# Two graph attention layers on one core: scores, projection, transposes, output projection, values in each step

## The chip, the core and the metric

The kernel runs on one core of a Trainium2 chip. The time is device microseconds of that core from one launch. Five engines work side by side and meet only through semaphores: TensorE (PE; its weight loads are shown as PEld) multiplies matrices into PSUM, VectorE (DVE), ScalarE (ACT) and GpSimd (POOL) do the rest, and SyncE (SP) issues the DMAs. Each engine takes its own instructions strictly in the order in which they are written.

## The reference, cut to what matters

128 graphs, 128 nodes each, 256 features, 8 heads of 32, float32. Two layers, each a masked attention over the nodes of a graph:

```python
# layer 0
nx = _ln(x, ln1_g, ln1_b)
q, k, v = nx @ wq + bq, nx @ wk + bk, nx @ wv + bv          # heads of 32
bias = jnp.where(adj > 0, 0.1 * adj * adj, -jnp.inf)[:, None]
attn = softmax(einsum('bhqd,bhkd->bhqk', q, k) / sqrt(32) + bias)
x1 = x + (einsum('bhqk,bhkd->bhqd', attn, v) @ wo + bo)
x  = x1 + gelu(_ln(x1, ln2_g, ln2_b) @ w1 + b1) @ w2 + b2    # 256 -> 1024 -> 256
# layer 1
q, k, v = x @ Wq + bq, x @ Wk + bk, x @ Wv + bv
attn = softmax(where(adj == 0, -inf, q k^T * scale))
y = x + (attn v) @ Wo + bo
out = (y - mean) * rsqrt(var + eps) * gamma + beta
```

## The kernel before, in words

The 128 graphs are worked on in 32 groups of four. Three stages run at once in one turn of a loop: A (layer 0's attention) of group n, M (the two-layer perceptron of layer 0) of group n-1, and C (layer 1) of group n-2. Turns 0, 1, 31, 32 and 33 are written out, the 29 between are a hardware loop. A turn has eight steps. Each step k computes the scores of one unit, that is one graph of one stage: steps 0 to 3 the four units of C, steps 4 to 7 the four of A. The rest of a unit's work follows in later steps, behind the scores of others. `lags` (line 61) says by how many steps: the transposes T of the probabilities one step later, the values V and the output projection W two steps later. A negative number is a unit of the previous turn.

What TensorE does in a step, in `body` (line 1399): the scores (`make_scores`, 16 small matmuls on 32 rows each, into `p_heads`), V of the unit two back (16 small matmuls 32 columns wide, stationary values, moving `probs_t`), the step's first projection ("early" and "mid": q, k or v of stage A or C, or the up-projection), T of the first four heads (`turn(.., 0)`), W of the unit two back, T of the other four heads, then "ahead" (the transposes XT of x before a projection) and "fill" (the second projection). Float32 products of the projections are three passes over a high and a low part of each operand (`three_passes`, line 1225, the multiply at line 1233). In step 3 the projection is the up-projection (UP, eight chunks of six matmuls) and half of DOWN, in step 4 the other half of DOWN.

The other engines, in the same step. VectorE (`body`, line 1060): adds the mask to the scores and takes the row bound (`mask_scores`, L925, eight instructions), inverts the sums of the exponentials (`invert`, L936), makes the low part of V's result (`heads_low`, L1005), adds W to the residual (`add_residual`, L1015), copies T's second half to `probs_t` (`turned`, L999), then the statistics of the layer norm (`measure`, L818 to L826) and, a step or more later, the normalised row (`apply_norm`, L832). ScalarE (`body`, line 752): V's high part (`heads_high`, L749), exps in two halves of four heads (L692), the copies of the projections, T's first half (L744), the high part of transposed x (L713). GpSimd (`body`, line 605): the multiply of the exponentials by the inverted sums (`make_probs`, L614, two halves), rstd (L560), the bias adds (`add_bias`, L592; the one into `res_c` at step 0 waits until all stores of the previous group are through), gamma and beta (`finish`, L601, L603). SyncE's stores of a finished unit wait for L603.

T writes the same PSUM banks as the scores, so each half of T waits until the masks of the newest scores in its banks are done, and for `make_probs`. Scores wait until the copies of earlier T are done. The four `p_bank`s are handed out in turn; each use waits until the use four before it is emptied (`take`, line 1207).

XT "M" in step 2 transposes the normalised `x_two` for the perceptron and needs all four of the turn's units through `apply_norm`: before, W of the last of them (A's unit 3) is in step 1.

Of the kernel before, what the change touches and what calls it, by code (L numbers as in the profile page):

```python
# [35 lines left out]
P = 128  # L36
# [3 lines left out]
HD = D // H  # L40
# [19 lines left out]

def lags(steps, pending, drain):
# [12 lines left out]
class Shape:  # L74
# [3 lines left out]
    def __init__(self, it, stages, following, before, drain):  # L78
# [10 lines left out]
        self.lag, self.tail = lags(self.steps, pending, drain)  # L89


        self.late, waiting = {}, [-3] if pending else []
# [24 lines left out]
        if it == NG:  # L117
            for table in (self.mid, self.fill, self.early):
                for k in (5, 6, 7):
                    table.pop(k, None)  # L120
            self.tail = self.tail[:3] + [("XH", "C", 0)] + self.tail[3:]
            self.ahead[4], self.fill[4] = [("KH", "C", 0), ("XH", "C", 1)], [("QH", "C", 0), ("KH", "C", 1)]
# [17 lines left out]
        for k in range(STEPS):  # L140
            lag = self.lag.get(k, [])
            self.number(self.first.get(k, []) + only("V", lag) + self.early.get(k, [])
                        + self.mid.get(k, []) + only("W", lag) + self.ahead.get(k, []) + self.fill.get(k, []))
# [8 lines left out]
        assert not self.looped or len(self.use) % BANKS == 0  # L152

# [37 lines left out]
class Turn:  # L191
# [32 lines left out]
    def high(self, key):  # L224

        return self.grown(self.s.high0 + self.s.high[key] + 1, len(self.s.high))
# [18 lines left out]
def build(nc, T, out):  # L245
    ctx = ExitStack()
    with ctx:
# [28 lines left out]
        piece_rooms = [sb(f"piece_room{i}", [P, 2, TOK]) for i in range(4)]  # L276
        scaled_rooms = [sb(f"scaled_room{i}", [P, 2, TOK]) for i in range(2)]
# [157 lines left out]
        def turned_rows(g):  # L435

            return probs_t[:, HC * g:HC * (g + 1)].rearrange("p (a h) n -> p a (h n)", a=2)
# [5 lines left out]
        def made(t, kind, what, i):  # L443
# [5 lines left out]
            return t.bank((kind, what, i), earlier=(what == "C" and not here))  # L449

# [14 lines left out]
        def _(sp):  # L465
# [36 lines left out]
            def body(t):  # L502
# [26 lines left out]
                if s.c:  # L529
                    store(t, 0)  # L530
                    store(t, 1)
# [3 lines left out]
                if s.c:  # L535
                    store(t, 2)
# [14 lines left out]
        def _(pool):  # L551
# [53 lines left out]
            def body(t):  # L605
                s = t.s
                setup_over(pool, t)
                for k in range(STEPS):
# [35 lines left out]
                    rstd_of(t, s.lag.get(k, []))  # L644
# [26 lines left out]
        def _(act):  # L671
# [69 lines left out]
            def turned(t, r):  # L741
                u, _, _ = t.unit(r)
                act.wait_ge(probs_turned, u * KC + 1)
                nc.scalar.activation(turned_rows(0), turned_columns(0), ACT.Copy).then_inc(turned_out0, 1)  # L744

            def heads_high(t, r):
                bank, number = t.bank(("O", r))
# [4 lines left out]
            def body(t):  # L752
                s = t.s
                setup_over(act, t)
                for k in range(STEPS):
# [19 lines left out]
                    for op in s.ahead.get(k, []):  # L775
                        evacuate(t, op)
                    for op in s.fill.get(k, []):
# [21 lines left out]
        def _(dve):  # L799
# [196 lines left out]
            def turned(t, r):  # L996
                u, _, _ = t.unit(r)
                dve.wait_ge(probs_turned, u * KC + 2)
                nc.vector.tensor_copy(turned_rows(1), turned_columns(1)).then_inc(turned_out1, 1)  # L999

            def heads_low(t, r):
                bank, _ = t.bank(("O", r))
                dve.wait_ge(high_made, t.high(("O", r)))
# [56 lines left out]
            def body(t):  # L1060
                s = t.s
                setup_over(dve, t)
                for k in range(STEPS):
                    lag = s.lag.get(k, [])
                    for op in s.first.get(k, []):
                        evacuate(t, op)
                        second_piece()
                    if k in s.units and k != s.behind:
# [3 lines left out]
                    for _, r in only("V", lag):  # L1072
# [18 lines left out]
                    for _, r in only("W", lag):  # L1091
                        add_residual(t, r)
                    for _, r in only("T", lag):
                        turned(t, r)
# [356 lines left out]
```

## Time and profile before

| | |
|---|---|
| median of 3 runs | 2177.07 us (2175.8 to 2178.03) |
| profiled execution | 2175.24 us, its span 2173.4 us |
| granted TensorE clock, mean | 0.998 |
| PE / PEld busy | 2138.1 us (98%) / 1853.7 us (85%) |
| DVE / ACT / POOL busy | 1802.9 (83%) / 1683.4 (77%) / 1153.3 us (53%) |
| 16 DMA engines | 75.76 MB, mean 35 GB/s |

A timeline row gives start, length, engine, line, operation, the tiles it writes and reads, and the count of merged instructions; the length runs to the end of the last one, which overlaps with the start of the next group. For the length of a TensorE group the difference of two starts is therefore used. A bracket at the end is idle time of the engine before the row, with what ended it.

### The profile page before, as it was taken

Reading aid. Unit: us, or ns where it says so; the run is one execution under the profiler, and the core shown is the slowest. Engines: PE = TensorE matmul, PEld = TensorE weight load, DVE = VectorE, ACT = ScalarE, POOL = GpSimd, SP = SyncE. Lnnn points to the kernel's source line nnn. Section 1 sums busy time; section 2 is a strip of 40 time slices with the busy share of each in tenths; the row PEclk is TensorE's granted clock in tenths of the full one; section 3 lists DMA queues with packets and bytes.
Section 4 is the critical chain, followed back from the end, with each engine's and each line's share of the span. In section 5 each row is a group of like instructions: output and inputs, shape, how many; then the busy total and the mean of one; then the engine's idle time right before and its main releaser. Section 6 shows DMA issues by size and latency. Waiting matters only on the chain.

```text
span 2173.4 us, 59064 instructions
## 1 busy us (share of the span) xinstructions
PE 2138.1 (98%) x20372; PEld 1853.7 (85%) x20372; DVE 1802.9 (83%) x8415; ACT 1683.4 (77%) x5658; POOL 1153.3 (53%) x1264
## 2 busy tenths in 40 slices
PE   8899999999999999999999999999999999999997
PEld 6888888888888888888888888888888888888876
DVE  7788888888888888888888888888888888888785
ACT  5678887778787778877787877787777788777875
POOL 4545555445655445555455554456554555544554
PEclk9999999999999999999999999999999999999999
DMA  4010111010111001111101110101111011101000
GB/s 130 30 33 26 40 33 40 26 35 28 40 33 40 24 29 38 34 40 31 31 28 41 33 40 26 35 28 40 33 32 32 27 40 33 40 27 34 19 26 18
DMA packets 94310, 75.76 MB, mean 35 GB/s; under 512 B 8129, under 2 KB 93761, under 8 KB 94017
## 3 DMA queue, kind: packets, MB, share of 16 engines
q1 hardware_dynamic: 94016, 71.99, 10.9%
q8 instruction: 167, 2.74, 0.5%
q14 instruction: 127, 1.03, 0.2%
HBM read 55.20 MB, written 16.78 MB: 33 GB/s over the span
## 4 chain that ended last, share of the span: by engine, by line
PE 96%; DVE 2%; ACT 1%; issue 1%; DMA 0%; POOL 0%; SPq 0%; POOLq 0%; DVEq 0%; ACTq 0%
PE p_bank L1233 67%; PE p_heads L1367 10%; PE p_heads L1354 8%; PE p_bank L1386 7%; PE p_bank L1266 4%; ACT scores L692 1%; DVE probs_t L999 0%; DVE normed L952 0%; PE p_bank L1156 0%; DMA scores<-in_L_gnn_wk 0%; DVE x_two L832 0%; DVE scores L925 0%; SPq L469 0%; DVE normed L946 0%; PE p_heads L1156 0%
## 5 line engine op out<-in xcount | busy, mean ns | idle before, releaser
L692 ACT ACTIVATE scores<-scores,negmax 128x128 f32<-128x128 f32 x2048 | 793.8, 392 | 23.3 <-DVE negmax L925 23.0
L614 POOL TENSOR_TENSOR scores<-scores,inverse 128x512 f32<-128x512 f32 x512 | 541.0, 1062 | 324.4 <-DVE inverse L936 324.4
L692 ACT ACTIVATION_READ_ACCUMULATOR scores<-scores,negmax 128x1 f32 x2048 | 391.9, 191 | 0.0
L1233 PEld LDWEIGHTS p_bank<-w_down,hidden 128*128 128x128 f32 x3072 | 374.6, 190 | 8.5 <-issue 5.9
L1233 PE MATMUL p_bank<-w_down,hidden 128*128 128x256 f32 x3072 | 381.8, 284 | 0.0
L1233 PE MATMUL p_bank<-normed,w_up 128*128 128x512 f32 (+1 forms) x1584 | 369.3, 389 | 3.6 <-DVE normed L946 2.9
L1233 PEld LDWEIGHTS p_bank<-normed,w_up 128*128 128x128 f32 x1584 | 286.2, 188 | 67.0 <-issue 10.2
L1367 PE MATMUL p_heads<-ident,scores 128*128 128x128 f32 x2048 | 309.7, 274 | 5.9 <-DVE negmax L925 3.3
L925 DVE CUSTOM_DVE_ANT_0 scores<-p_heads,adj_a 128x128 f32<-128x128 f32 x1024 | 235.2, 286 | 41.2 <-issue 41.2
L1367 PEld LDWEIGHTS p_heads<-ident,scores 128*128 128x128 f32 x2048 | 239.0, 140 | 31.6 <-DVE negmax L925 11.0
L735 ACT ACTIVATE p_bank<-p_bank,ready_cols 128x512 f32<-128x512 f32 x248 | 164.2, 662 | 126.9 <-PE p_bank L1233 121.5
L925 DVE CUSTOM_DVE_ANT_0 scores<-p_heads,adj_c 128x128 f32<-128x128 f32 x1024 | 233.2, 286 | 30.8 <-issue 30.8
L1233 PE MATMUL p_bank<-w_o,heads_t 128*128 128x256 f32 x1536 | 245.9, 296 | 2.4 <-DVE heads_t L1005 2.4
L749 ACT ACTIVATE heads_t<-p_bank 128x256 fp32r<-128x256 f32 x256 | 98.3, 384 | 159.6 <-PE p_bank L1386 159.5
L986 DVE TENSOR_TENSOR hidden<-p_bank,hidden 128x512 fp32r<-128x512 f32 x248 | 171.5, 691 | 60.6 <-ACT hidden L739 54.6
L744 ACT ACTIVATE probs_t<-p_heads 128x512 f32<-128x512 f32 x256 | 149.8, 585 | 87.2 <-PE p_heads L1367 87.2
L1233 PE MATMUL p_bank<-normed,w_k 128*128 128x512 f32 (+1 forms) x780 | 209.4, 404 | 4.2 <-DVE normed L952 2.6
L1233 PE MATMUL p_bank<-normed,w_q 128*128 128x512 f32 (+1 forms) x780 | 210.8, 406 | 0.0
L1233 PE MATMUL p_bank<-w_v,normed 128*128 128x256 f32 x1536 | 210.3, 287 | 0.0
L560 POOL TENSOR_TENSOR rstd_A<-spread_A,half 128x4 f32<-128x4 f32 x32 | 32.5, 1017 | 333.7 <-DVE spread_A L826 333.6
L1233 PEld LDWEIGHTS p_bank<-w_o,heads_t 128*128 128x128 f32 x1536 | 199.0, 190 | 3.2 <-DVE heads_t L1005 3.0
L1233 PEld LDWEIGHTS p_bank<-w_v,normed 128*128 128x128 f32 x1536 | 187.0, 189 | 12.5 <-issue 12.1
(130 smaller groups left out, 3708.1 us busy)
## 6 DMA issues: line engine op xcount, KB each, us to landing
res_a<-in_x SPq DMA_DIRECT2D x32, 512.0 KB, 3.8
out<-res_c SPq DMA_DIRECT2D x128, 128.0 KB, 1.7
x_in<-in_x SPq DMA_DIRECT2D x31, 512.0 KB, 3.9
adj_a<-in_adj SPq DMA_DIRECT2D x32, 256.0 KB, 2.9
adj_c<-in_adj SPq DMA_DIRECT2D x32, 256.0 KB, 2.9
piece_room<-in_L_gnn_w SPq DMA_DIRECT2D x2, 512.0 KB, 8.1
x_two<-in_x SPq DMA_DIRECT2D x1, 512.0 KB, 5.4
res_c<-in_L_gnn_w SPq DMA_DIRECT2D x1, 512.0 KB, 6.2
```

Source lines behind the costliest of these rows:

```text
L614: nc.gpsimd.tensor_tensor(rows_g, rows_g, inverse[:, step % 2, heads].unsqueeze(2).broadcast_to([P, HC, P]), ALU.mult).then_inc(probs_made, 1)
L692: last = nc.scalar.activation(scores[:, k % 2, h], scores[:, k % 2, h], ACT.Exp, scale=-1.0, bias=negmax[:, k % 2, h:h + 1], accum_out=tot ...
L735: nc.scalar.activation(src[:, :], src[:, :], ACT.Gelu, bias=ready_cols[:, 8 + j:9 + j]).then_inc(gelu_made, 1)
L744: nc.scalar.activation(turned_rows(0), turned_columns(0), ACT.Copy).then_inc(turned_out0, 1)
L749: nc.scalar.activation(heads_t[:, HI].rearrange("p c n -> p (c n)"), p_bank[bank][:, 0:KC * P], ACT.Copy).then_inc(high_made, 1)
L925: nc.vector.tensor_tensor_reduce(out=scores[:, k % 2, slot], in0=score_columns(c, j), in1=adj[stage][:, b, :], scale=1.0, scalar=LARGEST, ...
L986: nc.vector.tensor_tensor(hidden[:, j, LO, :], src[:, :], hidden[:, j, HI, :].bitcast(F32), ALU.subtract).then_inc(drained[bank], 1)
L1233: last = nc.tensor.matmul(dst, stationary(i), moving(j), start=(n == 0), stop=(n == total_n - 1))
L1266: last = nc.tensor.transpose(dst[:, b * P:(b + 1) * P], src[:, b, c * P:(c + 1) * P], ident[:, :])
L1354: last = nc.tensor.matmul(score_columns(c, j), queries[room(t, stage)][rows_j, c, tokens], keys[room(t, stage)][rows_j, c, tokens], start= ...
L1367: last = nc.tensor.transpose(turned_columns(g)[:, n // 2, (n % 2) * P:(n % 2 + 1) * P], scores[:, par, HC * g + n, :], ident[:, :])
L1386: last = nc.tensor.matmul(dst[HD * j:HD * (j + 1), c * P:(c + 1) * P], values[room(t, stage)][:, b, h * HD:(h + 1) * HD], probs_t[:, slot_ ...
```

## The change

From turn 1 to turn 32 the order of a step is another one (`later_lags`, `Shape.later`, `Shape.products`). T is still one step behind, V two, W now three. TensorE's order in a step is: scores, the step's projections, both halves of T together, W of the unit three back, V of the unit two back. Steps 2, 3, 4 and 7 differ where the transposes of x or the perceptron are in them (`products`). Since V of a unit now comes after T of the next one, the turned probabilities lie in two rooms, by the parity of the unit; the second is `piece_room0`, which is used only while weights are loaded. `heads_t` is written at the start of the step after V. In step 2 VectorE adds, measures and normalises A's unit 3 at once, and GpSimd's rstd comes ahead of `make_probs`. SyncE issues the load of `res_a` ahead of the stores 0 and 1. Turn 33 and turn 0 keep the old order.

```diff
+def later_lags(steps, pending, drain):
+    by_step = {}
+    for r, k in enumerate(steps):
+        by_step[k] = [(op, r - n) for op, n in (("T", 1), ("W", 3), ("V", 2)) if r >= n or pending]
+    last = len(steps) - 1
+    tail = [("T", last), ("W", last - 2), ("V", last - 1), ("XH", "C", 0), ("W", last - 1),
+            ("V", last), ("W", last)] if drain else []
+    return by_step, tail
...
+        self.later = before is not None and it != NG + 1
+        self.lag, self.tail = (later_lags if self.later else lags)(self.steps, pending, drain)
-        self.late, waiting = {}, [-3] if pending else []
+        self.late, waiting = {}, [-4] if pending else []
...
+    def products(self, k):
+        early, mid, ahead, fill = (x.get(k, []) for x in (self.early, self.mid, self.ahead, self.fill))
+        turns, outs, heads = (only(op, self.lag.get(k, [])) for op in "TWV")
+        if k == 2:
+            return early + outs + fill + turns + ahead + heads
+        if k == 3:
+            return mid + turns + outs + heads + ahead + fill
+        if k == 4:
+            return early + turns + ahead + outs + heads + fill
+        return ahead + early + mid + fill + turns + outs + heads
...
+        probs_rooms = [probs_t, piece_rooms[0][:, :, :].rearrange("p a (h n) -> p (a h) n", n=P)]
...
+        def turned_room(t, r):
+            return probs_rooms[0 if t.s.before is None else r % 2]
...  SyncE
-                if s.c:
-                    store(t, 0)
-                    store(t, 1)
                 if s.a and s.before is not None:
                     sp.wait_ge(*drained_use(t, ("DOWN", 1)))
                     sp.dma_start(res_a[:, :, :], ...)
                 if s.c:
+                    store(t, 0)
+                    store(t, 1)
                     store(t, 2)
...  GpSimd
+                    if k == 2 and s.later:
+                        rstd_of(t, s.lag.get(k, []))
                     if k in s.units and k != s.behind:
                         make_probs(k, 0)
...  ScalarE
-                    for _, r in only("V", lag):
+                    for r in split_first(s, k):
                         heads_high(t, r)
+                    for op in s.ahead.get(k, []) if s.later and k == 7 else []:
+                        evacuate(t, op)
...
+                    for op in s.fill.get(k, []) if s.later and k not in (3, 4) else []:
+                        evacuate(t, op)
                     for _, r in only("T", lag):
                         turned(t, r)
+                    for _, r in only("V", lag) if s.later and k == 3 else []:
+                        heads_high(t, r)
+                    for op in s.ahead.get(k, []) if s.later and k == 2 else []:
+                        evacuate(t, op)
                     if k in s.units and k != s.behind and not long:
                         exps(t, k, 1)
...  VectorE
+                    heads_lead = s.later and k == 2
+                    for r in split_first(s, k) if heads_lead else []:
+                        heads_low(t, r)
...
+                    if k == 2 and s.later:
+                        for _, r in only("W", lag):
+                            add_residual(t, r)
+                            measure(t, r)
                     if k == 2:
                         for r in s.late.get(k, []):
-                            apply_norm(t, r, GB - 1)
+                            apply_norm(t, r, GB - 2)
+                    for op in s.ahead.get(k, []) if s.later and k == 7 else []:
+                        evacuate(t, op)
...
+                    if s.later:
+                        if k == 2:
+                            for _, r in only("W", lag):
+                                apply_norm(t, r, GB - 1)
+                        for _, r in only("T", lag):
+                            turned(t, r)
+                        for op in s.ahead.get(k, []) if k in (2, 4) else []:
+                            evacuate(t, op)
+                        for _, r in only("W", lag) if k != 2 else []:
+                            add_residual(t, r)
+                        for _, r in only("V", lag) if k == 3 else []:
+                            heads_low(t, r)
...  TensorE
+                    if s.later:
+                        for op in s.products(k):
+                            if op[0] == "T":
+                                turn(t, op[1], 0)
+                                turn(t, op[1], 1)
+                            elif len(op) == 2 and op[0] in "VW":
+                                lagging(t, *op)
+                            else:
+                                work(t, op)
```

## Rows read from the trace of the kernel before

**Rows 1.** The page, first part: busy time, share of the span, instructions.

```profile
PE 2138.1 (98%) x20372; PEld 1853.7 (85%) x20372; DVE 1802.9 (83%) x8415; ACT 1683.4 (77%) x5658; POOL 1153.3 (53%) x1264
```

**Rows 2.** Waits of TensorE: engine, line, for whom; us, times, longest.

```profile
PE p_heads L1354 <- DVE probs_t L999: 3.7, 3, 1.7
```

**Rows 3.** Timeline of TensorE, step 0 to the scores of step 1.

```profile
238.83 0.73 PE L1354 MATMUL p_heads<-keys_c,queries_c 32*128 32x128 f32 x16
239.49 0.65 PE L1386 MATMUL p_bank<-probs_t,values_a 128*32 128x128 f32 x16
240.06 1.65 PE L1233 MATMUL p_bank<-normed,w_k 128*128 128x512 f32 x6
241.55 0.60 PE L1367 MATMUL p_heads<-ident,scores 128*128 128x128 f32 x4
241.91 0.96 PE L1233 MATMUL p_bank<-w_o,heads_t 128*128 128x256 f32 x6
...
243.06 1.64 PE L1233 MATMUL p_bank<-normed,w_k 128*128 128x512 f32 x6
244.63 0.73 PE L1354 MATMUL p_heads<-keys_c,queries_c 32*128 32x128 f32 x16
```

**Rows 4.** Timeline of TensorE, the same group in two turns.

```profile
130.44 8.50 PE L1233 MATMUL p_bank<-normed,w_up 128*128 128x512 f32 x36
...
196.55 8.50 PE L1233 MATMUL p_bank<-normed,w_up 128*128 128x512 f32 x36
```

**Rows 5.** Timeline of TensorE, DOWN after scores (turn 1) and ahead of values (turn 32).

```profile
79.59 6.01 PE L1233 MATMUL p_bank<-w_down,hidden 128*128 128x256 f32 x48
...
2118.95 5.91 PE L1233 MATMUL p_bank<-w_down,hidden 128*128 128x256 f32 x48
2124.80 0.64 PE L1386 MATMUL p_bank<-probs_t,values_c 128*32 128x128 f32 x16
```

**Rows 6.** Timeline of TensorE, values and projection in step 5.

```profile
221.10 0.64 PE L1386 MATMUL p_bank<-probs_t,values_c 128*32 128x128 f32 x16
221.79 1.62 PE L1233 MATMUL p_bank<-normed,w_k 128*128 128x512 f32 x6
```

**Rows 7.** Timeline of VectorE, step 7: first mask, residual add, statistics, spread.

```profile
299.10 0.29 DVE L925 CUSTOM_DVE_ANT_0 scores<-p_heads,adj_a 128x128 f32<-128x128 f32 x1 [0.65 <-issue]
...
302.36 0.42 DVE L1015 TENSOR_TENSOR res_a<-p_bank,res_a 128x256 f32<-128x256 f32 x1 [0.57 <-PE p_bank L1233]
...
303.41 0.42 DVE L818 BATCH_NORM_STATS2 stats_M<-res_a 128x6 f32<-128x256 f32 x1
...
304.08 0.15 DVE L826 TENSOR_SCALAR spread_M<-moments_M 128x1 f32<-128x1 f32 x1
```

**Rows 8.** Timeline of GpSimd, end of step 7 and step 0.

```profile
304.31 0.55 POOL L560 TENSOR_TENSOR rstd_M<-spread_M,half 128x1 f32<-128x1 f32 x1 [0.16 <-DVE spread_M L826]
304.83 1.28 POOL L592 TENSOR_TENSOR res_c<-x_two,row_bias 128x512 f32<-128x512 f32 x1
306.91 1.04 POOL L614 TENSOR_TENSOR scores<-scores,inverse 128x512 f32<-128x512 f32 x1 [0.80 <-DVE inverse L936]
```

**Rows 9.** Timeline of GpSimd and VectorE at the end of turn 0.

```profile
54.86 0.55 POOL L560 TENSOR_TENSOR rstd_M<-spread_M,half 128x1 f32<-128x1 f32 x1 [2.49 <-DVE spread_M L826]
55.37 2.39 POOL L398 TENSOR_TENSOR w_down<-x_in,w_down 128x1024 fp32r<-128x1024 f32 x1
...
55.44 2.47 DVE L832 TENSOR_SCALAR x_two<-res_a,moments_M,rstd_M 128x256 f32<-128x256 f32 x1 [0.66 <-POOL rstd_M L560]
```

**Rows 10.** Groups by line, ScalarE: busy us, mean ns; idle before, releaser.

```profile
L692 ACT ACTIVATE scores<-scores,negmax 128x128 f32<-128x128 f32 x2048 | 793.8, 392 | 23.3 <-DVE negmax L925 23.0
L713 ACT ACTIVATE normed<-p_bank 128x512 fp32r<-128x512 f32 x188 | 100.7, 588 | 40.4 <-PE p_bank L1266 40.4
```

**Rows 11.** Timeline of GpSimd, step 6: gamma of layer 1's last unit.

```profile
297.16 0.74 POOL L601 TENSOR_TENSOR res_c<-res_c,gamma 128x256 f32<-128x256 f32 x1
```

**Rows 12.** The page, DMA issues: count, KB, median us to landing.

```profile
out<-res_c SPq DMA_DIRECT2D x128, 128.0 KB, 1.7
```

More of the change, by code:

```diff
@@ L141, in __init__ @@
             lag = self.lag.get(k, [])
-            self.number(self.first.get(k, []) + only("V", lag) + self.early.get(k, [])
-                        + self.mid.get(k, []) + only("W", lag) + self.ahead.get(k, []) + self.fill.get(k, []))
+            if self.later:
+                self.number(self.products(k))
+            else:
+                self.number(self.first.get(k, []) + only("V", lag) + self.early.get(k, [])
+                            + self.mid.get(k, []) + only("W", lag) + self.ahead.get(k, []) + self.fill.get(k, []))
             if k == self.steps[-1]:
@@ L222, in normed_room, with high @@
         return (self.it + (what in "MN" or not self.s.m and self.s.c)) % 2
-    def high(self, key):
-        return self.grown(self.s.high0 + self.s.high[key] + 1, len(self.s.high))
+    def high(self, key, earlier=False):
+        s = self.s
+        n = s.before.high[key] - len(s.before.high) if earlier else s.high[key]
+        return self.grown(s.high0 + n + 1, len(s.high))
 def run_pipeline(eng, shapes, body):
@@ L449, in made, with split_first, out_use, out_high @@
             return t.bank((kind, what, i), earlier=(what == "C" and not here))
+        def split_first(s, k):
+            if s.later and k == 4:
+                return []
+            return [r for _, r in only("W" if s.later else "V", s.lag.get(k, []))]
+        def out_use(t, r):
+            taken_here = r >= 0 or ("V", r) in [op for ops in t.s.lag.values() for op in ops]
+            return t.bank(("O", r)) if taken_here else t.bank(("O", r + len(t.s.before.order)), earlier=True)
+        def out_high(t, r):
+            if r >= 0 or ("O", r) in t.s.high:
+                return t.high(("O", r))
+            return t.high(("O", r + len(t.s.before.order)), earlier=True)
         def second_turn(t):
@@ L643, in body @@
                         add_bias("A", res_a_loaded, (t.group_a + 1) * 16, 1, 1)
-                    rstd_of(t, s.lag.get(k, []))
+                    if k != 2 or not s.later:
+                        rstd_of(t, s.lag.get(k, []))
                     if k == 3 and second_turn(t):
@@ L1071, in body @@
                         invert(t, k - 1, 1)
-                    for _, r in only("V", lag):
+                    for r in split_first(s, k) if not heads_lead else []:
                         heads_low(t, r)
@@ L1097, in body @@
                             evacuate(t, op)
-                    for _, r in only("W", lag):
+                    for _, r in only("W", lag) if not (s.later and k == 2) else []:
                         measure(t, r)
-                    if k == 1:
-                        for r in s.late.get(k, []):
-                            apply_norm(t, r, 2)
-                    for op in s.ahead.get(k, []):
+                    for op in s.ahead.get(k, []) if not (s.later and k in (2, 4, 7)) else []:
                         evacuate(t, op)
@@ L1408, in body @@
                         make_scores(t, k)
+                    if s.later:
[5 more added lines that the diff above has]
+                                lagging(t, *op)
+                            else:
+                                work(t, op)
+                        for op in s.tail if k == s.steps[-1] else []:
+                            if len(op) == 2 and op[0] in "TVW":
+                                lagging(t, *op)
+                            else:
+                                work(t, op)
+                        continue
                     for op, r in only("V", lag):
```

34 lines of the change are left out of this document (17 added, 17 removed).

## The prediction

> **What bounds the kernel now.** First the page's busy shares: TensorE's matmuls are busy 98% of the span [rows 1]; the chain that ended last is nearly all TensorE too. Then the list of who waited for whom, for TensorE: its longest entry is 3.7 us in the whole run, in three waits, all in the last turns [rows 2]. Then the timeline of a step: TensorE's groups follow each other without an idle gap [rows 3]. And the period: the 36 UP matmuls that start at 130.44 come again at 196.55 [rows 4], 66.1 us later, and so on through the loop. So the time is the length of TensorE's own stream. Other engines matter only when they make it stop, and today they hardly do. A change of order can therefore win only what changing from one kind of matmul to another costs, and loses every wait that it creates.
>
> I count from the profiled execution: 2175.24 us, span 2173.4. The median of the timed runs is 1.8 us higher; I add that at the end.
>
> **The price of changing the kind.** An ordinary step is scores S (0.66), values V (0.57), six large matmuls K (1.49), transposes T (0.355), output projection W (0.80), T, K (1.57 with the first of them after T) [rows 3]. K unhindered is 1.38 (half of the 2.86 that twelve take). So K after V pays 0.11, and K ahead of S 0.09. T and W change places at next to nothing: 0.355 + 0.80 is what ten such matmuls take in a row. S and V are tiled (32 rows; 32 columns), and entering or leaving them is what costs; the change S to V pays about 0.11 + 0.02 of the same kind. DOWN directly after S lasts 6.01, 0.10 longer than after UP (5.91): entering the full array costs the same after S as after V. And those 48 matmuls, 0.12 each, take 5.85 up to the V that follows them [rows 5], 0.09 of it for leaving, as ahead of S. So leaving costs about 0.1 whatever follows, and entering belongs to what is entered.
>
> With that the new steps come out so. Old: full array to S, S to V, V to full: three changes. New: S to full, full to V, V to next S: again three, and by the rows above the same 0.55 us. Only step 3 (S, UP, T, W, V, UP, DOWN) has one more exit and entry: 0.2 us a turn. Merged transposes save 0.005 eight times, step 7 enters x transposes instead of a projection after S (0.05 less), and in step 5 today's wait of K for the split of x (V group 0.69 instead of 0.57 [rows 6]) goes, 0.12. Sum: 0.2 - 0.04 - 0.05 - 0.12, nothing. The one change that no row shows is V to S. Its bounds: free (0.21 less, seven times a turn) to 0.1 more; I take it as S to V, the nearest row.
>
> The Trainium skill, TensorEngine Tiling (Array Packing), Key Properties, says that changing the tiling mode, not just the tile, drains the engine. By it V to S is such a change as well, and the ring stays equal; this trace shows the drain at S to V and at V to full.
>
> **Step 2: a new wait.** W of a turn's last layer-0 unit moves from step 1 to step 2, and the transposes of x (X) in the same step need that unit normalised. Counted from the start of step 2's scores: S 0.66, first half of v 1.48, so W runs 2.14 to 2.85; second half 1.37, eight transposes 0.87 (0.109 each, four T take 0.355 up to W and 0.08 more of its first): X could start at 5.10. VectorE: step 1's measuring now comes after W, at step end, and is over at 0.9; ScalarE's and its own part of the heads 0.4 each; masks start near 1.4 and eight of them at 0.21 with a reciprocal end at 3.2. Residual add 0.42, statistics to spread 0.82 (303.41 to 304.08 + 0.15) [rows 7], spread ready at 4.5. GpSimd starts rstd 0.08 later and takes 0.55 [rows 8], 0.67 with VectorE on a normalise: 5.2. Then comes the collision. GpSimd's next instruction is the multiply of step 2's first four heads, 1.04 [rows 8], whose reciprocals VectorE has made at 5.0, and it starts back to back; VectorE's normalise needs the rstd and starts 0.07 later. The end of turn 0 shows just this [rows 9]: rstd to 55.41, GpSimd's next from 55.37 for 2.39, VectorE's normalise from 55.44 for 2.47 instead of 0.41: it ended 0.15 after GpSimd. So here it ends at 5.2 + 1.04 + 0.15 = 6.4, X starts at 6.44, and TensorE stands **1.3 us**. Without the collision: 5.27 + 0.41 + 0.06 = 5.74, 0.64 us. If VectorE runs half a microsecond ahead of my count the latter shrinks to 0.1; behind it, 1.6. I take 1.3.
>
> The Trainium skill, SBUF — State Buffer, section "SBUF: two separate sides", calls the port pair of VectorE and GpSimd an exclusive lock, held for the whole instruction by whichever starts first. By that rule the wait is 1.3, without it 0.64; the trace agrees, 2.47 us at 55.44.
>
> **Step 3.** ScalarE now copies x (two copies of 0.59, overlapping to 1.09) [rows 10] before the second half of step 2's exps. From X's start x0: copies 0.86 to 1.95, four exps at 0.39 plus a last read, to 3.55, heads high 0.3, heads low 0.36, so step 3's masks run 4.24 to 6.0. TensorE: V starts x0 + 1.04, V 0.57, S 0.66, UP 2.86, first four transposes 0.44, second four at 5.57; these write the banks that the masks read. **0.5 us**, between 0 and 0.8. Before, the same transposes came after W, at the scores' start + 5.2, and the masks ended at 3.9. UP needs x's split at x0 + 2.27 and has it at 2.2: nothing.
>
> **Step 0.** The last layer-1 unit is now projected in step 6 and finished by GpSimd in step 7, where before it had step 6 for that [rows 11]. From step 7's scores: ScalarE copies x_in to 2.65, exps to 4.25, GpSimd's multiply 4.55 to 5.65, gamma and beta 0.75 each to 7.2, bias of res_a 1.28 to 8.45, rstd 0.55 to 9.0; the store of res_c lands at 7.25 + 1.7 to 2.0 [rows 12]. The bias add into res_c waits for that store: 9.0 to 10.4 (1.28) [rows 8], and only then comes the multiply for the second four heads, 11.4. Step 7 lasts 6.6, so it is ready 4.8 after step 0's scores start; the second four transposes would go at 0.66 + 2.86 + 0.44 = 3.96. Before, it was ready at 306.91 + 1.04 = 307.95, 3.0 after scores at 304.95, for transposes at 3.87. **0.8 us**, between 0 (everything 0.8 earlier) and 1.2.
>
> **Edits that cost nothing.** The second room for turned probabilities is memory that is idle after the start. S waits for the copies of turned probabilities; VectorE's starts 0.2 after the transposes (4.6) and ends at 5.3, scores at 5.8: 0.4 spare, covered by W and V. The residual add and the measuring then end at 0.8 of the next step, just when its masks can start (0.80 after the scores, [rows 7], scores at 298.30); any more would move the masks, whose user (3.96) is 0.9 behind their end. In step 4 W and V stand between the transposes of x and the next scores and hide the split. SP's queue: the res_a load is moved ahead of two stores that now finish later; it is needed in step 5. The banks of W and V are free a step ahead. Turn 32 has no projections to hide step 2's chain: 3 us once. The last turn keeps the old order.
>
> **Sum.** Steps 0 and 2 in 30 turns: 30 x (0.8 + 1.3) = 63; step 3 in 31 turns 15.5; turn 32 3: 81.5 us. 2175.2 + 81.5 = 2256.7, and with the 1.8 of the median 2258; I give 2255.
>
> **The rivals.**
> A, chance 0.30: part of it. The waits in steps 0 and 3 come out hidden, because a wait in one place gives every engine time to catch up for the next, and VectorE gets the ports first in step 2: 31 x 0.64 = 20, to 31 x (1.3 + 0.5) = 56. 2185 to 2232, middle 2205. For it: my chains have three to six terms each, and an error of 0.3 in VectorE's start removes half a wait. Against: at 55.4 the same two engines met in the same order [rows 9].
> B, chance 0.09: the waits are all hidden and the ring is equal: 2177. For it: today's VectorE has some 0.65 idle ahead of masks [rows 7]. Against: step 2's chain has 2.4 us of fixed latency from W's end, against 2.25 us of TensorE's work.
> C, chance 0.13, the other side: V to S is free, both being tiled. Place: seven of eight step borders. Price 0.21 each, 1.5 us a turn, 46 us. It decides from where the waits are less than 1.5 us a turn: with step 2's 0.64 alone 2177 + 20 - 46 = 2151; with all of mine, 2.6 a turn, even it leaves the kernel slower. Against: at S to V, also between two tiled kinds, the full price stands.
> The forecast has 0.48, own range 2232 to 2285.
>
> What a measurement can tell from no change is about 0.2%, 4.4 us. Faster 0.13 (C), same 0.09 (B), slower 0.78 (forecast, A). The range must reach from the forecast over A to B to leave out no more than C and a little above: 2174 to 2285.
>
> **What would show it.** In the profile after: TensorE's waits should name x_two's normalise (L832) before the transposes of x, some 30 times at 1.3; negmax before transposes in step 3 at 0.5; GpSimd's scores multiply before transposes in step 0 at 0.8, with GpSimd's res_c add waiting for a store. The step 2 normalise should last about 1.1 instead of 0.41. The turn should be 68.7 us. A V group that is 0.57 long with S right behind shows the equal price; 0.45, rival C. If the turn is 66.1 and no such waits are listed, my schedule of VectorE and GpSimd is wrong, not the prices.

## The result, and the profile after

The changed kernel takes 2265.81 us (median of 4 runs, 2264.55 to 2267.68) against 2177.55 us (4 runs, one more than in the table ahead of the prediction, 2175.8 to 2179.3) beside it: ratio 1.041, 95% interval 1.0397 to 1.0422, 88 us slower. The profiled execution has a span of 2265.9 us at a mean granted clock of 0.991.

The page of the changed kernel, first part (answers to [rows 1]):

```profile
PE 2169.0 (96%) x20372; PEld 1876.7 (83%) x20372; DVE 1851.6 (82%) x8415; ACT 1684.1 (74%) x5658; POOL 1155.8 (51%) x1264
```

The first entries of TensorE's list of waits (engine, line, for whom; us, times, longest; answers to [rows 2]):

```profile
PE p_bank L1347 <- DVE x_two L894: 34.3, 32, 2.2
PE p_heads L1448 <- issue: 24.5, 32, 1.9
PE p_heads L1448 <- DVE negmax L987: 10.3, 37, 1.1
```

The number of instructions is that of before on every engine. TensorE's share of the span fell by two points only, and the page alone would hide where 88 us went. The list of waits has it: before, the longest entry was 3.7 us in three waits; now three entries have a wait in nearly every turn (32, 32 and 37 times), 69 us in sum. L1347 is the transposes of x, L894 the normalise; L1448 the transposes of probabilities, L987 the masks. The entry in the middle is step 0's wait. The list puts it down to "issue", that is, to nothing that the profile shows, and not to GpSimd's multiply of the probabilities, as the prediction expected; that the multiply is the cause rests on the rows and edits told at e2 and e5.

Timeline of TensorE in the changed kernel, steps 2 and 3 of one turn:

```profile
953.08 1.04 PE L1448 MATMUL p_heads<-ident,scores 128*128 128x128 f32 x8
955.16 1.09 PE L1347 MATMUL p_bank<-ident,x_two 128*128 128x128 f32 x8 [1.04 <-DVE x_two L894]
956.19 0.64 PE L1467 MATMUL p_bank<-probs_t,values_c 128*32 128x128 f32 x16
956.76 0.73 PE L1435 MATMUL p_heads<-keys_c,queries_c 32*128 32x128 f32 x16
957.54 3.00 PE L1314 MATMUL p_bank<-normed,w_up 128*128 128x512 f32 x12
960.38 0.60 PE L1448 MATMUL p_heads<-ident,scores 128*128 128x128 f32 x4
961.17 0.66 PE L1448 MATMUL p_heads<-ident,scores 128*128 128x128 f32 x4 [0.19 <-DVE negmax L987]
961.59 0.96 PE L1314 MATMUL p_bank<-w_o,heads_t 128*128 128x256 f32 x6
...
963.05 8.52 PE L1314 MATMUL p_bank<-normed,w_up 128*128 128x512 f32 x36
```

The same, step 0 of the next turn, and the UP group one turn later (answers to [rows 3] and [rows 4]):

```profile
1005.11 0.73 PE L1435 MATMUL p_heads<-keys_c,queries_c 32*128 32x128 f32 x16
1005.77 3.03 PE L1314 MATMUL p_bank<-normed,w_k 128*128 128x512 f32 x12
1008.63 0.60 PE L1448 MATMUL p_heads<-ident,scores 128*128 128x128 f32 x4
1009.79 0.63 PE L1448 MATMUL p_heads<-ident,scores 128*128 128x128 f32 x4 [0.56 <-issue]
1010.18 0.96 PE L1314 MATMUL p_bank<-w_o,heads_t 128*128 128x256 f32 x6
...
1031.64 8.52 PE L1314 MATMUL p_bank<-normed,w_up 128*128 128x512 f32 x36
```

A group's length is the difference of two starts. Eight merged transposes take 0.79 where nothing holds them (shown at e5). In step 2 they take 953.08 to 955.16, 2.08: a wait of 1.29. In step 3 it is 960.38 to 961.59, 1.21: 0.42 waited. In step 0 1008.63 to 1010.18, 1.55: 0.76. Scores of step 3 take 0.78 instead of 0.66 (up-projection waits for the split of x): 0.12. Sum 2.59 us. The turn is 1031.64 - 963.05 = 68.59 (median of all turns 68.58, before 66.11), so without waits it would be 66.0. By this count all of the 2.47 us that a turn got longer are waits.

Between the spans lie 92.5 us: 30 turns at 2.47 are 74.0; the period that ends with turn 32's UP is 5.8 longer (62.77 to 68.60); behind that UP come 1.6 more (62.8 to 64.4); the first UP of turn 1 comes 6.3 us later (66.13, before 59.84); and 4.7 sit in a few turns, the longest 71.41. At 252, 939, 1626 and 2040 the wait of step 0 is 0.7 to 1.3 longer than in the others (3.9 in sum), because of a late store (told at e5); behind the third the clock falls. That the first UP comes late is, as far as I can see, the clock too (last section).

The 5.8 us of turn 32 are not step 2's chain alone. TensorE's granted clock falls twice there, behind idle times of 1.90 us (step 0) and 2.17 us (step 2): it is 0.56 in the mean from 2192.5 to 2196.4, and in no stretch of that turn does it fall in the kernel before.

```profile
2192.55 1.83 PE L1347 MATMUL p_bank<-ident,x_two 128*128 128x128 f32 x8 [2.17 <-DVE x_two L894]
```

These transposes of x take 1.76 us to the next group, where an ordinary turn has 1.03 (955.16 to 956.19); the values behind them take 1.02 instead of 0.57. Behind the 1.90 us, W takes 1.27 instead of 0.88 and the values 1.01 instead of 0.57. Together these four groups are 2.0 us longer at the lower clock.

### The profile page after: what moved, and what is told of

It reads as the page before. It is cut to its first block, busy times and chain, and to the rows that moved or that the text cites. A ratio compares the mean times of both kernels' runs of the same rounds, so it can differ in the third digit from the quotient of the medians.

```text
span 2265.9 us, 59064 instructions
## 1 busy us (share of the span) xinstructions
PE 2169.0 (96%) x20372; PEld 1876.7 (83%) x20372; DVE 1851.6 (82%) x8415; ACT 1684.1 (74%) x5658; POOL 1155.8 (51%) x1264
## 3 DMA queue, kind: packets, MB, share of 16 engines
q14 instruction: 126, 1.03, 0.2%
## 4 chain that ended last, share of the span: by engine, by line
PE 77%; DVE 10%; ACT 9%; issue 3%; POOL 1%; DMA 0%; SPq 0%; POOLq 0%; DVEq 0%; ACTq 0%
PE p_bank L1314 55%; PE p_heads L1448 7%; PE p_heads L1435 5%; PE p_bank L1467 5%; ACT scores L746 5%; PE p_bank L1347 4%; DVE scores L987 3%; DVE x_two L894 2%; ACT normed L767 1%; DVE heads_t L1067 1%; POOL rstd_M L611 1%; ACT queries_a L772 1%; ACT heads_t L803 1%; DVE negmax L987 1%; ACT probs_t L798 1%
## 5 line engine op out<-in xcount | busy, mean ns | idle before, releaser
L1448 PE MATMUL p_heads<-ident,scores 128*128 128x128 f32 x2048 | 280.8, 275 | 35.3 <-issue 24.5
L1448 PEld LDWEIGHTS p_heads<-ident,scores 128*128 128x128 f32 x2048 | 232.8, 141 | 74.5 <-issue 31.5
L987 DVE CUSTOM_DVE_ANT_0 scores<-p_heads,adj_c 128x128 f32<-128x128 f32 x1024 | 233.1, 286 | 7.0 <-issue 7.0
L987 DVE CUSTOM_DVE_ANT_0 scores<-p_heads,adj_a 128x128 f32<-128x128 f32 x1024 | 233.2, 286 | 2.2 <-issue 2.2
L1048 DVE TENSOR_TENSOR hidden<-p_bank,hidden 128x512 fp32r<-128x512 f32 x248 | 168.7, 690 | 59.2 <-ACT hidden L793 55.0
L611 POOL TENSOR_TENSOR rstd_C<-spread_C,half 128x1 f32<-128x1 f32 x128 | 70.6, 552 | 262.9 <-DVE spread_C L888 262.9
L1314 PE MATMUL p_bank<-w_v,normed 128*128 128x256 f32 x1536 | 202.6, 285 | 0.0
L1314 PE MATMUL p_bank<-normed,w_k 128*128 128x512 f32 (+1 forms) x780 | 195.9, 400 | 2.5 <-DVE normed L1014 2.1
L1314 PE MATMUL p_bank<-normed,w_q 128*128 128x512 f32 (+1 forms) x780 | 195.0, 399 | 0.0
L767 ACT ACTIVATE normed<-p_bank 128x512 fp32r<-128x512 f32 x188 | 102.1, 595 | 94.5 <-PE p_bank L1347 94.5
```

Source lines behind the costliest of these rows:

```text
L611: nc.gpsimd.tensor_tensor(rstd[n][:, b0:b1], spread[n][:, b0:b1], half[:, b0:b1], ALU.pow).then_inc(rstd_made[n], 1)
L767: nc.scalar.activation(normed[t.normed_room(what)][:, HI, use[2], :], src[:, :], ACT.Copy).then_inc(high_made, 1)
L987: nc.vector.tensor_tensor_reduce(out=scores[:, k % 2, slot], in0=score_columns(c, j), in1=adj[stage][:, b, :], scale=1.0, scalar=LARGEST, ...
L1048: nc.vector.tensor_tensor(hidden[:, j, LO, :], src[:, :], hidden[:, j, HI, :].bitcast(F32), ALU.subtract).then_inc(drained[bank], 1)
L1314: last = nc.tensor.matmul(dst, stationary(i), moving(j), start=(n == 0), stop=(n == total_n - 1))
L1448: last = nc.tensor.transpose(turned_columns(g)[:, n // 2, (n % 2) * P:(n % 2 + 1) * P], scores[:, par, HC * g + n, :], ident[:, :])
```

## Experiments

They ask three things: is each of the three waits caused as predicted, are the three separate, and what does a change of kind cost TensorE. Turn means the median period of the UP group.

**Normalise ahead of the multiply (e1).** GpSimd's multiply in step 2 waits until A's unit 3 is normalised.

```diff
                     if k == 2 and s.later:
                         rstd_of(t, s.lag.get(k, []))
+                        if k in s.units:
+                            pool.wait_ge(ln_applied["M"], (t.group_m + 1) * GB)
```

> The changed kernel, but in step 2 GpSimd takes up its multiply of the first four heads only after VectorE has normalised the last layer-0 unit. Theory (collision): the 1.21 us that TensorE stands ahead of the transposes of x is 0.65 collision and 0.55 latency of the chain from W. Then the normalise falls from 1.05 to 0.41 us, the wait to about 0.55, and the time by 31 x 0.65 = 20 us, to 2246. Rival (latency alone, the multiply only runs beside it): no change, 2266.

Measured: 2246.27 us (2242.36 to 2252.46), ratio to before 1.0319 (1.0297 to 1.0341); turn 67.95, 0.63 less. The changed kernel, timeline of GpSimd in step 2, then of VectorE:

```profile
953.93 1.03 POOL L665 TENSOR_TENSOR scores<-scores,inverse 128x512 f32<-128x512 f32 x1
```

```profile
954.06 1.05 DVE L894 TENSOR_SCALAR x_two<-res_a,moments_M,rstd_M 128x256 f32<-128x256 f32 x1 [0.42 <-POOL rstd_M L611]
```

And e1, the same place: GpSimd, VectorE, TensorE:

```profile
940.52 0.67 POOL L611 TENSOR_TENSOR rstd_M<-spread_M,half 128x1 f32<-128x1 f32 x1 [1.02 <-DVE spread_M L890]
...
941.79 1.04 POOL L665 TENSOR_TENSOR scores<-scores,inverse 128x512 f32<-128x512 f32 x1 [0.60 <-DVE x_two L896]
```

```profile
941.30 0.41 DVE L896 TENSOR_SCALAR x_two<-res_a,moments_M,rstd_M 128x256 f32<-128x256 f32 x1 [0.43 <-POOL rstd_M L611]
```

```profile
940.32 1.04 PE L1450 MATMUL p_heads<-ident,scores 128*128 128x128 f32 x8
941.76 1.09 PE L1349 MATMUL p_bank<-ident,x_two 128*128 128x128 f32 x8 [0.41 <-DVE x_two L896]
```

The same instruction takes 1.05 us when GpSimd's has started 0.13 before it and 0.41 when it goes first; TensorE's wait falls from 1.29 to 941.76 - 940.32 - 0.79 = 0.65. The multiply starts 1.47 after the transposes of probabilities instead of 0.85, 0.6 later, and costs nothing. So half of the wait is the collision and half is the chain from W over the statistics and rstd.

**The multiply ahead of the bias add (e2).** In step 0 GpSimd multiplies the second four heads first and adds the bias into `res_c` after.

```diff
+                    if k in s.open:
+                        make_probs(k - 1, 1)
                     if k == 0 and s.c:
                         wait(pool, stored, t.group_c * GB * 16)
...
                         add_bias("C", drained[bank], number, 0, 1)
-                    if k in s.open:
-                        make_probs(k - 1, 1)
```

> The changed kernel, but in step 0 GpSimd multiplies the last unit's second four heads before it adds the bias into res_c. Theory: the 0.72 us in front of the second four transposes of step 0 is GpSimd's order (late gamma and beta, store, bias add, then the multiply); it goes whole, 30 x 0.72 = 22 us, time 2244. Rival (the transposes wait for VectorE's masks or for the exps behind them): it stays, 2266, or only a part goes.

Measured: 2262.67 us (2260.03 to 2266.86), 1.0393 (1.0376 to 1.0411); turn 68.63, no gain. A miss. The wait is gone from the transposes and has come up one group later. Waits of TensorE in e2:

```profile
PE p_heads L1435 <- DVE piece_room L1061: 26.0, 33, 1.6
```

The scores of step 1 wait for VectorE's copy of the turned probabilities (0.74 us at 1007.24). VectorE's normalise stands ahead of that copy and waits 1.26 us, until 1005.13, for the bias add, which now comes later still. Changing the order on GpSimd only chose which of its users is late; the lateness came from further up.

**The exponentials ahead of the copy of x (e3).** On ScalarE, step 2.

```diff
-                    for op in s.ahead.get(k, []) if s.later and k == 2 else []:
-                        evacuate(t, op)
                     if k in s.units and k != s.behind and not long:
                         exps(t, k, 1)
+                    for op in s.ahead.get(k, []) if s.later and k == 2 else []:
+                        evacuate(t, op)
```

> The changed kernel, but in step 2 ScalarE takes the second four exps before it copies the transposed x. Theory: the 0.35 us in front of step 3's second transposes comes from the exps that wait behind the copy, while ScalarE is idle for 1.7 us; it goes, 31 x 0.35 = 11 us, time 2255. Rival: the exps now delay the copy of x and with it the up-projection; nothing gained, 2266 or more.

Measured: 2247.13 us (2246.17 to 2251.82), 1.0324 (1.0308 to 1.034); turn 68.15, 0.43 less, and TensorE waits for masks 4.0 us in the run instead of 10.3. The median is 18.7 us lower and the turns give 13 of it; in the profiled executions the first UP comes 6.2 earlier, which the edit doesn't touch (last section). ScalarE in the changed kernel has room for it:

```profile
956.07 1.08 ACT L767 ACTIVATE normed<-p_bank 128x512 fp32r<-128x512 f32 x2 [1.71 <-PE p_bank L1347]
957.05 0.40 ACT L746 ACTIVATE scores<-scores,negmax 128x128 f32<-128x128 f32 x1
```

It stood idle for 1.71 us ahead of the copy, with four exponentials (1.6 us) behind it whose inputs were ready.

**All three (e4).** The diffs of e1, e2 and e3 together.

> The three moves together. Theory: the waits are separate and add up: 2266 - 20 - 22 - 11 = 2213, what is left being 0.55 us a turn in step 2 and about 0.2 of further changes of kind. Rival (a wait removed in one place comes back in the next, since the other engines have less time to catch up): 2225 to 2245.

Measured: 2237.81 us (2236.68 to 2243.88), 1.0276 (1.0258 to 1.0293); turn 67.90. The rival held. Waits of TensorE:

```profile
PE p_heads L1437 <- DVE piece_room L1063: 23.3, 33, 1.0
...
PE p_bank L1316 <- DVE normed L1016: 14.2, 32, 1.5
```

The first is e2's moved wait. The third entry of that list, 14.2 us, is the price of e3 once X comes earlier: the up-projection waits for VectorE's low part of x, which needs the high part, and ScalarE now copies that after the exponentials.

**The root of step 0's wait (e5).** The last C unit is normalised in step 7 ahead of VectorE's split of x_in, and GpSimd's gamma and beta go ahead of that step's multiply.

```diff
+                    if s.later and k == 7:
+                        for r in s.late.get(k, []):
+                            finish(t, r)
...
-                        finish(t, r)
+                        if not (s.later and k == 7):
+                            finish(t, r)
...
+                    early_late = s.later and k == 7
+                    for r in s.late.get(k, []) if early_late else []:
+                        apply_norm(t, r, None)
```

> The changed kernel, but in step 7 the last unit of layer 1 is normalised ahead of VectorE's split of x_in, and GpSimd's gamma and beta for it go ahead of that step's multiply of the probabilities; the order of step 0 stays. Theory (the last store of layer 1 is the root of the wait of the second transposes in step 0, and putting the multiply ahead of the bias add only moved it to VectorE's copy): the 0.72 us of step 0 goes and nothing takes its place, the turn is 67.9 us instead of 68.58, and the time 2244. Rival (the wait moves again, or GpSimd is late anyway): turn 68.6, time 2263.

Measured: 2236.29 us (2233.75 to 2238.12), 1.0268 (1.0254 to 1.0282); turn 67.82. GpSimd in the changed kernel:

```profile
1002.91 1.12 POOL L665 TENSOR_TENSOR scores<-scores,inverse 128x512 f32<-128x512 f32 x1 [1.54 <-DVE inverse L998]
...
1004.81 0.74 POOL L654 TENSOR_TENSOR res_c<-res_c,beta 128x256 f32<-128x256 f32 x1
...
1007.40 1.30 POOL L643 TENSOR_TENSOR res_c<-x_two,row_bias 128x512 f32<-128x512 f32 x1
1008.65 1.04 POOL L665 TENSOR_TENSOR scores<-scores,inverse 128x512 f32<-128x512 f32 x1
```

And e5, GpSimd and then TensorE in step 0 (scores at 987.12):

```profile
984.65 0.74 POOL L654 TENSOR_TENSOR res_c<-res_c,beta 128x256 f32<-128x256 f32 x1
...
989.80 1.04 POOL L665 TENSOR_TENSOR scores<-scores,inverse 128x512 f32<-128x512 f32 x1
```

```profile
990.64 1.04 PE L1455 MATMUL p_heads<-ident,scores 128*128 128x128 f32 x8
991.43 0.95 PE L1321 MATMUL p_bank<-w_o,heads_t 128*128 128x256 f32 x6
```

Counted from the scores of step 0, beta ends 1.7 before them instead of 0.4 after, the late multiply ends at +3.7 instead of +4.6, and the eight transposes take 0.79: no wait, and none came up elsewhere. The prediction had the bias add wait for the store, and e2's and e5's theories did too. In an ordinary turn of the changed kernel it hardly does: it starts 0.1 after rstd, behind a queue with no gap above 0.1 since 1002.91, so the queue explains its start but for about 0.13 us (in the kernel before and in e5 it starts 0.03 ahead of the end of rstd). What these 0.13 us wait for no row shows. The store decides in a few turns only, as at 1626 in the changed kernel:

```profile
1625.87 1.27 POOL L643 TENSOR_TENSOR res_c<-x_two,row_bias 128x512 f32<-128x512 f32 x1 [1.44 <-DMA out<-res_c]
```

In all it is four turns (0.83, 1.08, 1.44 and 1.08 us of GpSimd's idle time). In e5 GpSimd waits for these stores 2.0 us in the whole run, of which 1.8 is in one wait that the kernel before has too. Its time is 29.5 us lower: 0.76 x 30 is 22.8, 3.9 were late stores, and 2.8 are left. I can't split these in the medians. In the profiled executions, which lie 32.5 apart, the first UP comes at 59.2 and not at 66.1 and the clock doesn't fall in the loop (1.5), while the end behind turn 32's UP is 1.9 longer.

**Without the moved wait of e2 (e6).** e1, e3 and e5 together.

> The changed kernel with three edits at once: the normalisation of x ahead of GpSimd's multiply in step 2, the exponentials ahead of ScalarE's copy of x in step 2, and the early normalisation of layer 1's last unit in step 7 in place of the exchanged bias add of step 0. Theory (the three waits are separate, and what the kernel with all three first edits kept was the wait that the exchanged bias add made): turn 67.1 us, time 2214; what is left is 0.57 us in step 2 and 0.35 to 0.47 us of an up-projection that waits for the split of x. Rival (the waits are the load of VectorE and ScalarE over the turn and turn up elsewhere): turn above 67.5 us.

Measured: 2214.54 us (2213.33 to 2215.74), 1.0169 (1.0155 to 1.0183); turn 67.13. The theory gave 67.1 and 2214. TensorE in step 2 and at the start of step 3:

```profile
995.02 1.04 PE L1457 MATMUL p_heads<-ident,scores 128*128 128x128 f32 x8
996.43 1.09 PE L1356 MATMUL p_bank<-ident,x_two 128*128 128x128 f32 x8 [0.37 <-DVE x_two L900]
...
998.03 0.73 PE L1444 MATMUL p_heads<-keys_c,queries_c 32*128 32x128 f32 x16
999.18 3.00 PE L1323 MATMUL p_bank<-normed,w_up 128*128 128x512 f32 x12 [0.43 <-DVE normed L1020]
```

What is left is 0.62 ahead of the transposes of x (1.41 - 0.79) and 0.49 at the up-projection (1.15 - 0.66). 67.13 - 1.11 = 66.02: with waits taken off, this order is within 0.1 us of the old one, whose turn is 66.11 with its own 0.12 of waiting in step 5 [rows 6].

**One change of kind less (e7).** The values of step 3 go to the end of the step, directly ahead of step 4's scores; with them ScalarE's and VectorE's parts of their result go to the start of step 4 (those lines are not in the diff below).

```diff
+        if k == 3 and 4 in self.units:
+            return mid + turns + outs + ahead + fill + heads
```

> The changed kernel, but the values of step 3 are issued at the end of the step, directly ahead of step 4's scores, so that TensorE changes the kind of its work three times there and not four. Theory (each change of kind costs about 0.2 us by itself): turn 68.38 us instead of 68.58, time about 6 us below the changed kernel's. Rival (a change of kind costs nothing itself, the longer groups are waits): no change, within 1 us.

Measured: 2257.38 us (2253.37 to 2261.36), 1.0368 (1.0351 to 1.0384); turn 68.53, 0.05 less, in some turns 68.38. TensorE in one of the latter:

```profile
954.56 0.95 PE L1316 MATMUL p_bank<-w_o,heads_t 128*128 128x256 f32 x6
955.35 8.41 PE L1316 MATMUL p_bank<-normed,w_up 128*128 128x512 f32 x36
963.60 5.91 PE L1316 MATMUL p_bank<-w_down,hidden 128*128 128x256 f32 x48
```

W takes 0.79 instead of 0.88 (961.59 to 962.47 in the changed kernel), UP 8.25 instead of 8.36 (963.05 to 971.41): leaving the full array is 0.09, entering it 0.11, and both are gone, 0.20 as expected in these turns. In 22 of 30 turns UP takes 8.40 instead of 8.25, and this gives three quarters of it back. I don't know what makes those 0.15 us; the list of waits does not name them. The median turn therefore misses the 68.38 of the theory. The median time's 8.4 us are mostly not the edit: 30 x 0.05 is 1.5, and the first UP comes 4.5 earlier.

**Values ahead of scores in the kernel before (e8).** No other part of the change is in it.

```diff
                     if k in s.units:
-                        make_scores(t, k)
...
+                    if k in s.units:
+                        make_scores(t, k)
```

> The kernel before, with the values ahead of the scores in every step, so that all borders between the two go from values to scores and nothing else of the change is there. Theory (a border costs the same in both directions): the values' group stays at 0.57 us and the scores' at 0.66, the turn stays near 66.1 us, the time 2177 to 2192 (the masks come 0.57 us later, which may cost up to 0.5 us a turn in step 5). Rival (going from values to scores is free): turn 64.5 us, time 2130 to 2145.

Measured: 2184.92 us (2183.4 to 2186.22), 1.0032 (1.0019 to 1.0044); turn 66.30. TensorE in e8, step 6:

```profile
1024.49 0.64 PE L1386 MATMUL p_bank<-probs_t,values_a 128*32 128x128 f32 x16
1025.06 0.73 PE L1354 MATMUL p_heads<-keys_a,queries_a 32*128 32x128 f32 x16
1025.72 1.66 PE L1233 MATMUL p_bank<-normed,w_q 128*128 128x512 f32 x6
```

Values take 0.57 and scores 0.66, as in the other order [rows 3]. In step 5 scores take 0.77 (1019.13 to 1019.90), which has the 0.11 that the values had there before [rows 6]: the projection waits for x whichever group stands ahead. The 0.19 us a turn that e8 does cost are not where I had put up to 0.5 (masks, step 5) but at the end of step 0, where the second half of the k projection takes 1.76 instead of 1.57 up to the values. The trace of e8 has the reason: the values' first weight load starts at 1042.89, 0.11 behind the end of VectorE's copy of the turned probabilities (1042.10 + 0.68), which they read. Ahead of the scores the values come 0.66 us sooner in the step, and the copy is no longer done in time.

## Why the prediction was right

It gave 2255 us, range 2174 to 2285; the time is 2266. Its own sum was 2256.7 and 1.8, so 2258.5; the 3.5 below that have no reason. The 2.6 us of waits a turn were right, and each of the three waits came where it was put.

- **Step 2: 1.3 predicted, 1.29 measured; 0.64 without the collision predicted, 0.65 in e1.** The normalise took 1.05, predicted about 1.1. [Rows 9] had shown the same normalise at 55.44 beside another, longer multiply of GpSimd, and the count of the chain had put GpSimd's multiply back to back with its rstd, which is what decides. The Trainium skill, SBUF — State Buffer, section "SBUF: two separate sides", says that the shared port pair goes to whichever of VectorE and GpSimd starts first, for the whole instruction; the trace agrees on who is delayed, 1.05 us behind GpSimd's start and 0.41 ahead of it. That the other stands wholly still it does not show: the normalise ends 0.15 us after the multiply (953.93 + 1.03, 954.06 + 1.05), less than the 0.41 that it takes alone.
- **Step 3: 0.5 predicted, 0.42 measured.** Cause as told: e3 takes it away (0.43) by letting the exponentials go ahead of the copy.
- **Step 0: 0.8 predicted, 0.76 measured.** The chain (multiply, gamma and beta, bias adds, late multiply) ran as counted, 0.2 us earlier at its end (4.6 after the scores instead of 4.8). e5 shows its root in step 7. One sign failed: the bias add was to wait for a store, and GpSimd's waits have that in four turns only (and once where the kernel before has it too); the store, which the prediction had land about when rstd ends, came 0.8 to 1.4 late in four turns. The term didn't need it, since the end of rstd in GpSimd's queue gives the 9.0 as well.
- **The ring of changes of kind: nothing predicted; without waits 66.0 against 66.11.** Values to scores costs what scores to values does (e8: 0.57 and 0.66), so rival C, 46 us of gain, fails: its turn would have been 64.5, e8's is 66.30. The extra exit and entry of step 3 is 0.20, as predicted, in the 8 of 30 turns where e7 shows it whole. The unhindered K of 1.38 is not half of 2.86, as it says (that is 1.43); it comes out if 0.11 for entering is taken off first, and e7's UP, 8.25 for 36 or 1.375 for six, bears it out. The Trainium skill, TensorEngine Tiling (Array Packing), Key Properties, says that changing the tiling mode drains the engine; e8 agrees for the direction that the trace of before did not have, in that scores behind values take 0.66 us, no less than behind the full array. The drain itself no row shows.
- **What was left out.** The up-projection of step 3 waits 0.12 for the split of x; the prediction had it ready 0.07 ahead. Turn 32 was put at 3 us, and the period that ends with its UP is 5.8 longer, of which about 2.0 are the two falls of the clock, which the prediction did not have; what is left, 3.8, is near its 3 and 0.5. And 6.3 us before the first UP, 4.7 in a few turns and 1.6 behind turn 32's UP had no term. The prediction's terms were 81.5 us; in their places the profile has 74.0 + 5.8 = 79.8. That the two are so close is in part luck: the 30 turns came out 4.0 under their 30 x 2.6, and turn 32 made up for a good half of it, mostly by the clock. The profiled time lies 11.0 above the prediction's 2256.7: 12.6 that had no term, less the 1.7.
- **Rivals A and B** (waits partly or wholly hidden because another wait lets every engine catch up) fail: the three do not help each other in the changed kernel. (A's lower end of 2185 did not follow from its own terms, 2177 + 20.) Where a wait did vanish by another's presence it was in the repairs: e1, e2 and e3 took 0.63, nothing and 0.43 off the turn, and together 0.68 instead of 1.06, with a new wait for the split of x.

Repaired as far as e6, the new order is still 37 us slower than the kernel before, 1.11 us a turn in two waits. Without them it would come out about equal (an estimate from the 66.02), since the ring gains nothing; so I tried no further version of it.

## What to carry to other kernels

Where one engine is 98% busy and follows its own order without a gap, a new order can win only the changes of kind that it saves: count them first, with both directions at the full price, and then follow each other engine's chain to the new places. When two engines share a lock, ask which one's instruction is issued a tenth of a microsecond earlier, and give the one on the critical path the start. A wait that is moved by swapping two instructions has its root further up the queue: look for what makes the whole queue late.

## What the runs showed of the hardware

**The clock in the start.** Granted clock in stretches of the first 66 us (us, TensorE busy and instructions, clock, DMA share, GB/s); the kernel before, then the changed one:

```profile
20.00:30.00 10.00, 6.80 (x81) 1.00 0.80 244
30.00:46.00 16.00, 13.58 (x145) 1.00 0.06 17
```

```profile
20.00:30.00 10.00, 7.80 (x74) 1.00 0.79 245
30.00:46.00 16.00, 12.65 (x96) 0.57 0.01 2
```

Both run the same order of work there (turn 0 keeps the old one). The changed kernel spent most of 30 to 46 at the lower level (1.2 of 2.4 GHz); TensorE was busy 7.8 of the 10 us ahead of that, in the kernel before 6.8. 16 us at a mean of 0.57 are 6.9 us of full clock lost, an estimate from this row, and the first UP came 6.3 later. e3, e5 and e7 had their first UP at 59.9, 59.2 and 61.7 again, with no edit in the start. So I take it that some 4 to 6 us of a difference between two kernels with such a start can be the clock alone (no run changed the clock by itself), and a gain under that has to be read from the period of a turn and not from the time.

**The clock behind a long wait.** In the loop it fell once each in the changed kernel, e1, e2 and e3 (stretches of 4 us looked at one by one), every time right behind one of that run's longest waits. TensorE in the changed kernel, where the scores take 1.16 instead of 0.66, and the clock of the stretch:

```profile
1628.24 0.63 PE L1448 MATMUL p_heads<-ident,scores 128*128 128x128 f32 x4 [1.87 <-issue]
...
1630.52 1.24 PE L1435 MATMUL p_heads<-keys_c,queries_c 32*128 32x128 f32 x16
1631.68 2.69 PE L1314 MATMUL p_bank<-normed,w_q 128*128 128x512 f32 x8
```

```profile
1619.00:1629.00 10.00, 8.13 (x79) 1.00 0.35 94
1629.00:1633.00 4.00, 4.00 (x40) 0.57 0.01 2
```

The idle time ahead was 1.87 here, 2.13 in e1, 1.51 in e2 and 2.31 in e3; the changed kernel lost 1.5 us by it. Not each such wait does it: e1 has another as long at 925.7 with the clock at 1.00 behind it. e5, without these waits, has no such fall from 70 to 2140; the kernel before has none there either. In turn 32 of the changed kernel it falls twice, behind 1.90 and 2.17 us (told in the section on the result). So a wait can cost more than its length.

**Which exchange is free.** A GpSimd multiply of 1.03 us can be put off by 0.6 us with no loss, while its being 0.13 us ahead costs TensorE 0.64 us in every turn. By the busy shares (POOL 51%, DVE 82%) neither engine looks as if its order mattered.
